# Edge ranking in 80 half-target buckets, and count matmuls of one half per chunk, in a two-layer graph network kernel

## What is computed

```python
edge_index = jnp.stack([src, dst])                    # 20625 edges, 625 nodes
xn = _layernorm(x, axis=-1)
x = x + _L0_gnn_ref(xn, edge_index, edge_type_8, ...) + _L0_mix_ref(xn[None], ...)[0]
x = x + _L0_ffn_ref(_layernorm(x, axis=-1)[None], ...)[0]
xn = _layernorm(x, axis=-1)
x = x + _L1_gnn_ref(xn, edge_index, ...) + _L1_mix_ref(xn[None], ...)[0]
x = x + _L1_ffn_ref(_layernorm(x, axis=-1)[None], ...)[0]
```

```python
for r in range(8):
    mask = (edge_type == r)
    sums = jax.ops.segment_sum(msgs * mask[:, None], dst, num_segments=n)
    cnt = jax.ops.segment_sum(mask, dst, num_segments=n)
    out = out + (sums / jnp.maximum(cnt, 1.0)[:, None]) @ weight[r]
```

## Time and profile before

| | |
|---|---|
| runs | 1880.85 us median of 3 (1880.52 to 1880.96) |
| profiled execution | span 1878.8 us, from first to last instruction |
| PE busy | 1794.9 us (96%) |
| PEld busy | 1477.4 us (79%) |
| DVE busy | 1023.3 us (54%) |
| ACT busy | 478.5 us (25%) |
| POOL busy | 701.1 us (37%) |

### The profile page before, as it was taken

How to read it: one execution, slowest core, us unless ns; L and a number is a source line. 1 busy time by engine, 2 the same in 40 slices (tenths; PEclk the granted TensorE clock), 3 DMA queues, 4 the chain that set the end, 5 groups by cost and what they waited for, 6 DMA issues and landing times.

```text
span 1878.8 us, 28666 instructions
## 1 busy us (share of the span) xinstructions
PE 1794.9 (96%) x9953; PEld 1477.4 (79%) x9953; DVE 1023.3 (54%) x2540; ACT 478.5 (25%) x1055; POOL 701.1 (37%) x609
## 2 busy tenths in 40 slices
PE   6999999999999999999999999954999999999999
PEld 4876689987777778787777887742899888878987
DVE  7888999997254543526354356786632224362311
ACT  3139956662010110101011145243100000111100
POOL 2110000003634435353534444200485552345862
PEclk9999999999999999999999999956999999999999
DMA  4532222224213121231313534110354351113322
GB/s 134 154 109 77 73 86 79 75 67 129 91 38 89 45 72 56 66 86 47 94 33 113 172 84 131 45 46 7 96 164 146 104 156 51 37 55 118 90 73 66
DMA packets 129282, 162.23 MB, mean 86 GB/s; under 512 B 14288, under 2 KB 75368, under 8 KB 128922
## 3 DMA queue, kind: packets, MB, share of 16 engines
q1 hardware_dynamic: 100848, 120.93, 21.5%
q10 hardware_dynamic: 22250, 23.53, 4.0%
q0 software_dynamic: 6080, 16.40, 2.9%
HBM read 135.51 MB, written 25.30 MB: 86 GB/s over the span
## 4 chain that ended last, share of the span: by engine, by line
PE 84%; DVE 6%; ACT 6%; issue 1%; DVEq 1%; DMA 1%; POOL 0%; ACTq 0%; SPq 0%
PE ps L367 22%; PE ps L368 22%; PE ps L369 21%; PE ps L1236 9%; PE ps L892 3%; ACT sc_col L838 2%; ACT sc_row L837 1%; PE ps L1201 1%; DVE w_lo L318 1%; PE ps L881 1%; PE ps L1156 1%; DMA nat<-in_x 1%; ACT w_hi L313 1%; PE ps L1183 1%; PE ps L1211 0%
## 5 line engine op out<-in xcount | busy, mean ns | idle before, releaser
L367 PE MATMUL ps<-w_hi,xt_hi 128*125 128x512 f32 x1320 | 539.0, 408 | 9.1 <-DVE xt_lo L549 3.5
L256 POOL TENSOR_TENSOR w_hi<-w_stage,zero 128x512 fp32r<-128x512 f32 x256 | 276.8, 1081 | 684.4 <-PE ps L369 670.0
L368 PE MATMUL ps<-w_lo,xt_hi 128*125 128x512 f32 x1320 | 523.0, 396 | 0.0
L369 PE MATMUL ps<-w_hi,xt_lo 128*125 128x512 f32 x1320 | 521.5, 395 | 0.0
L259 POOL TENSOR_TENSOR w_lo<-w_stage,w_hi 128x512 fp32r<-128x512 f32 x256 | 346.2, 1352 | 20.1
L367 PEld LDWEIGHTS ps<-w_hi,xt_hi 128*125 128x125 f32 x1320 | 246.6, 187 | 67.1 <-DVE xt_lo L549 4.3
L369 PEld LDWEIGHTS ps<-w_hi,xt_lo 128*125 128x125 f32 x1320 | 246.0, 186 | 63.3
L368 PEld LDWEIGHTS ps<-w_lo,xt_hi 128*125 128x125 f32 x1320 | 246.3, 187 | 53.5
L367 PE MATMUL ps<-xt_hi,w_hi 128*128 128x314 f32 x736 | 250.5, 340 | 1.3 <-DVE ring L2430 0.6
L369 PE MATMUL ps<-xt_hi,w_lo 128*128 128x314 f32 x736 | 225.9, 307 | 0.0
L368 PE MATMUL ps<-xt_lo,w_hi 128*128 128x314 f32 x736 | 225.7, 307 | 0.0
(11 more groups left out here) (392 smaller groups left out, 2390.2 us busy)
## 6 DMA issues: line engine op xcount, KB each, us to landing
w_stage<-in_stream SPq DMA_DIRECT2D x374, 256.0 KB, 2.7
pre<-ring POOLq DMA_DIRECT2D x30, 250.0 KB, 3.8
a_qt<-pre_t SPq DMA_DIRECT2D x18, 312.5 KB, 3.8
a_qt<-pre_t ACTq DMA_DIRECT2D x14, 312.5 KB
pre_t<-ring_t POOLq DMA_DIRECT2D x12, 312.5 KB, 2.8
pre_t<-ring_t ACTq DMA_DIRECT2D x12, 312.5 KB
a_vx<-pre SPq DMA_DIRECT2D x9, 312.5 KB
nat<-pre SPq DMA_DIRECT2D x2, 1250.0 KB
```

The costliest lines, as they stand in the source:

```text
L256: POOL.tensor_tensor(w_hi[:, q, :], w_stage[:, q % NST, :], zero[:].to_broadcast([128, 512]), ALU.add).then_inc(S("hi_done"), 1)
L367: PE.matmul(dst, l_hi, r_hi, start=first, stop=False)
L368: PE.matmul(dst, l_hi, r_lo, start=False, stop=False)
L369: return PE.matmul(dst, l_lo, r_hi, start=False, stop=last)
```

## The change

- A bucket is now relation, source tile and half of the targets (`SPLIT` = 314): 80 buckets (`NKEY`), rounded up to chunks of 128 slots, again 240 chunks. Targets are numbered within their half. A chunk's counts have 314 columns.
- Ranking: three buckets, 28 apart, share one row of `key_hot` as fields of 8 bits (weights 1, 256, 65536), so that table and running sum have 28 x 166 = 4648 elements. New are `key_weight` (`key_hot` times the edge's weight), the unpacking of sums, `ranks()` (rank of each edge within its partition, ahead of the evacuation of group 1), `rank_fields()`, and in `positions` 80 scalar operations (`key_start`, int16) in place of one addition and one multiplication of 6600 elements.
- Counts: for each chunk one `hot_col` of 314 targets and one count matmul of 314 columns; `hot_row` for four chunks at a time in one operation of 512 elements (`iota1_by4`), read by PE with a stride of four columns; the two chunks of a pair go to two banks (6 and 7, or 4 and 5) and are copied by one ACT operation of 2 x 314; two adds of 314 instead of one of 626; packed words of three chunks instead of four groups. DVE makes the hot_col of chunk c+4 ahead of the add of chunk c.

```diff
-GROUP = 256
-NGROUP = (EDGES + NBUCKET * (GROUP - 1)) // GROUP
-NCHUNK = 2 * NGROUP
+SPLIT = 314
+NKEY = 2 * NBUCKET
+FIELDS, NROW = 3, 28
+CHUNK = 128
+NCHUNK = (EDGES + NKEY * (CHUNK - 1)) // CHUNK
...
-        for b in (0, half):
-            DVE.tensor_tensor(key_hot[:, b:b + half], e_key[:].unsqueeze(1).to_broadcast([P, half, EC]),
-                              iota16[0:P, b:b + half].unsqueeze(2).to_broadcast([P, half, EC]), ALU.is_equal)
-            if b == 0:
-                split_low_dve(8, 11)
+        DVE.tensor_tensor(key_hot[:], e_row[:].unsqueeze(1).to_broadcast([P, NROW, EW]),
+                          iota16[0:P, 0:NROW].unsqueeze(2).to_broadcast([P, NROW, EW]), ALU.is_equal)
+        split_low_dve(8, 11)
+        DVE.drain()
+        DVE.tensor_tensor(key_weight[:], key_hot[:], e_weight[:].unsqueeze(1).to_broadcast([P, NROW, EW]), ALU.mult)
         evacuate(0)
...
+    def ranks():
+
+        DVE.tensor_tensor(scan[:], scan[:], key_hot[:], ALU.mult)
+        DVE.drain()
+        n = NROW
+        while n % 2 == 0:
+            n //= 2
+            DVE.tensor_tensor(scan[:, 0:n], scan[:, 0:n], scan[:, n:2 * n], ALU.add)
+            DVE.drain()
+        DVE.tensor_reduce(e_rank[:], scan[:, 0:n].rearrange("p b c -> p c b"), AX.X, ALU.add)
+        DVE.drain()
...
     def positions(evacuate):
-        DVE.tensor_tensor(scan[:], scan[:], b_off[:].unsqueeze(2).to_broadcast([P, NBUCKET, EC]), ALU.add)
-        DVE.tensor_tensor(scan[:], scan[:], key_hot[:], ALU.mult)
+        for b in range(NKEY):
+            DVE.tensor_scalar(key_start[:, b, :], e_key16[:], float(b), b_off[:, b:b + 1], ALU.is_equal, ALU.mult)
+            if b == NKEY // 2:
+                split_low_dve(24, 27)
...
+    def hist_hot(c):
+        if c % 4 == 0:
+            if c >= 8:
+                DVE.wait_ge(S("hi_pe"), c - 4)
+            DVE.tensor_tensor(hot_row[c // 4 % 2][:], iota1_by4[:],
+                              slot_row[:, c:c + 4].unsqueeze(1).to_broadcast([128, 128, 4]), ALU.is_equal)
+        if c >= 8:
+            DVE.wait_ge(S("hi_pe"), c - 7)
+        DVE.tensor_scalar(hot_col[c % 8][:], iota1_16[:, 0:SPLIT], slot_col[:, bass.ds(c, 1)], None,
+                          ALU.is_equal).then_inc(S("hi_dve"), 1)
+
+    def hist_copy(g):
+        b = pair_bank(g)
+        ALE.wait_ge(S("hi_pe"), 2 * g + 2)
+        if g >= 4:
+            ALE.wait_ge(S("hi_add"), 2 * g - 6)
+        ALE.activation(counts[g % 4][:], ps[0:P, b:b + 2, 0:SPLIT], ACT.Copy).then_inc(S("hi_main"), 1)
+
+    def hist_add(c, packed):
+        bucket = (packed >> (7 * (c % 3))) & 127
+        start = nc.s_assert_within((bucket >> 1) * NB + (bucket & 1) * SPLIT, 0, (NBUCKET - 1) * NB + SPLIT,
+                                   skip_runtime_bounds_check_because="a bucket's number is below NKEY")
+        DVE.wait_ge(S("hi_main"), c // 2 + 1)
+        if c:
+            DVE.wait_ge(S("hi_add"), c)
+        o = adj[:, bass.ds(start, SPLIT)]
+        DVE.tensor_tensor(o, o, counts[c // 2 % 4][:, c % 2, :], ALU.add).then_inc(S("hi_add"), 1)
...
         mk = bucket_counts(evacuate)
         split_low_dve(16, 21)
+        ranks()
         dense(1)
         mk = bucket_sums(mk)
         evacuate(1)
         split_low_dve(21, 24)
-        mk = group_buckets(mk)
+        rank_fields()
+        mk = chunk_buckets(mk)
```

More of the change, by code:

```diff
@@ L682, in build @@
     assert r_hot + sc_per * 1248 <= R_NAT + T * D * 4
[L683 to L688, removed]
+    slot_col = tmp("slot_col", [128, NCHUNK], F32, 1)
+    slot_row = tmp("slot_row", [128, NCHUNK], F16, 1)
+    hot_col = [tmp(f"hot_col{i}", [128, SPLIT], F16, 1) for i in range(8)]
+    hot_row = [tmp(f"hot_row{i}", [128, 128, 4], F16, 1) for i in range(2)]
+    zero16 = tmp("zero16", [P, 2 * NCHUNK], F16, 1)
+    iota1_by4 = at("iota1_by4", [128, 128, 4], F16, r_hot + sc_per * 1248)
+    assert r_hot + sc_per * 1248 + 1024 <= R_NAT + T * D * 4
+    counts = [at(f"counts{i}", [P, 2, SPLIT], I16, R_NAT + i * 1280) for i in range(4)]
     slot_ps = ps[:, 5, 0:2 * NCHUNK]
@@ L715, in bucket_counts @@
         DVE.tensor_scalar(e_key[:], ed_typ[:], float(T), None, ALU.mult)
+        DVE.scalar_tensor_tensor(e_col1[:, 0:EC], e_half[:], -float(SPLIT), e_col1[:, 0:EC], ALU.mult, ALU.add)
         DVE.drain()
@@ L811, in packed_buckets @@
         gflat = gcol[:].rearrange("o g j -> o (g j)")
[L812 removed]
+        DVE.tensor_scalar(gflat, ps[0:1, 6, 0:NCHUNK], -1.0, None, ALU.add)
         DVE.drain()
@@ L860, in hist_copy @@
-    def hist_copy(g, gm):
-        b4, b1 = group_banks(gm)
-        ALE.wait_ge(S("hi_pe"), 8 + 2 * g + 2)
-        ALE.wait_ge(S("hi_add"), g + 1)
-        ALE.activation(counts[gm][:, C1:NB], b1, ACT.Copy).then_inc(S("hi_rest"), 1)
-        ALE.activation(counts[gm][:, 0:C1], b4, ACT.Copy).then_inc(S("hi_main"), 1)
-    def hist_dve_add(g, gm, packed):
-        bucket = nc.s_assert_within((packed >> (6 * gm)) & 63, 0, NBUCKET - 1,
-                                    skip_runtime_bounds_check_because="a bucket's number is below NBUCKET")
-        DVE.wait_ge(S("hi_rest"), 2 + g + 1)
-        DVE.wait_ge(S("hi_main"), 2 + g + 1)
-        DVE.wait_ge(S("hi_add"), 4 + g)
-        o = adj[:, bass.ds(bucket * NB, NB)]
-        DVE.tensor_tensor(o, o, counts[gm][:], ALU.add).then_inc(S("hi_add"), 1)
@@ L877, in hist_pe_rest @@
[L877 to L893 removed]
+    LEAD_HOT = 4
@@ L895, in beside, with hist_pe @@
+    def hist_pe(g):
+        if g >= 2:
+            PE.wait_ge(S("hi_main"), g - 1)
+        if g == 1:
+            PE.wait_ge(S("bank_free"), (SC0 + SC_GROUPS + 1) * T)
+        for j in range(2):
+            c = 2 * g + j
+            PE.wait_ge(S("hi_dve"), c + 1)
+            PE.matmul(ps[0:P, pair_bank(g) + j, 0:SPLIT], hot_row[c // 4 % 2][:, 0:P, c % 4], hot_col[c % 8][:],
+                      start=True, stop=True).then_inc(S("hi_pe"), 1)
+    SC0, LEAD = 4, 6
     def beside(dense, evacuate, evacuate_half, load_bias):
@@ L923, in beside @@
         PE.sem_inc(S("sc_pe"), sc_per)
-        PE.sem_inc(S("hi_pe"), 6)
-        zero16 = hot_col[4][0:P, 0:128]
-        DVE.memset(zero16, 0.0)
-        DVE.memset(hot_col[5][0:P, 0:2 * NCHUNK], 0.0)
-        DVE.memset(slot[:, :, NCHUNK:NCHUNK + 4], 0.0)
-        for q in (6, 7):
-            DVE.memset(hot_col[q][:], 0.0)
-            DVE.memset(hot_row[q][:], 0.0)
+        DVE.memset(zero16[:], 0.0)
+        DVE.tensor_copy(iota1_by4[:], iota1_16[:, 0:128].unsqueeze(2).to_broadcast([128, 128, 4]))
         mk = sig(DVE.drain(), "dve_step")
         wait(PE, mk)
-        PE.matmul(slot_ps, zero16, hot_col[5][0:P, 0:2 * NCHUNK], start=True, stop=False)
+        PE.matmul(slot_ps, zero16[:, 0:128], zero16[:], start=True, stop=False)
         def scatter_step(i):
```

219 lines of the change are left out of this document (124 added, 95 removed).

## The result

The changed kernel takes 1972.08 us (median of 4 runs, 1970.87 to 1972.81), the kernel before, run beside it, 1880.68; the ratio is 1.0488 with a 95% interval from 1.0473 to 1.0503. The forecast said slower, with 1920 us and a range up to 1948: the direction held, the size did not. The measured loss is 91 us where 39 were forecast.

The account below looks back on a forecast made before the run. DVE was taken to set the count stage's pace, with PE close behind. Span 1878.8 + 12 (ranking) - 1 (before the count stage) + 29 (count stage) + 2.05 (outside the span) = 1920.9, stated as 1920 us; range 1885 to 1948.

Parts of the forecast that it names:

- Ranking and clock: Ranking stage: PE waits for late evacuations, then runs at a lower clock (+1.7 us); scatter starts 12 us later (6 to 18).
- The engines' share of the count stage: Count stage: DVE and PE, taken as engines alone, would allow some 150 us instead of 181.5.
- rival 1: Count stage: sequencer's work stays hidden, engines bind at 150 us; kernel 1861 us; chance 0.15.
- the period of 0.80 and 0.90 us: Count stage: time from add to add on DVE, 0.80 us without a load, 0.90 with one; mean 0.83.
- the high end, 0.85: Count stage: upper estimate of the period from add to add without a load, 0.85 us.
- 12 us that the forecast added for splits: Count stage: 32 w_lo splits on DVE are not covered between adds and lengthen the stage by 12 us.
- Rival 2: Count stage: sequencer's work half hidden, period 0.70 us, stage 179 us; kernel 1886 us; chance 0.07.
- Rival 3: Count stage: PE's clock drops and PE sets the pace for a quarter of the pairs; +20 us, 1940; chance 0.08.
- Rival 4: Ranking costs nothing, count stage as forecast; kernel 1909 us; chance 0.70 together with the main forecast.
- lower end of 1898: Whole kernel: low end, 1898 us, of the span 1898 to 1938 given for the main forecast.
- What would show it: Signs expected in the trace: count stage near 210 us, adds 0.8 apart, DVE near 60% busy, PE pausing some 9 us.
- The signs of being wrong: Count stage: adds at 0.6 us or PEclk low across it; ranking: key_start operations at 0.3 us each, +8 more.

Follow-up runs that it names:

- e5_resched: Changed kernel with DVE's ranking order changed: evacuation 1 ahead of the halvings in ranks(), evacuation 2 behind 65 key_start operations, splits moved to match; 1962.82 us.
- e2_static: Changed kernel with add addresses known when it is built: no register steps, no packed words loaded, wait kept, counts in wrong blocks; 1858.63 us.
- e3_load_once: Changed kernel with 2 packed-word loads instead of 80; most register steps fell away too, most counts land in wrong blocks; 1860.27 us.
- e1_regs_first: Changed kernel with each add's address computed into its own register ahead of the two waits, only base plus offset left behind; 1949.9 us.

## Why the prediction was right in direction and too small

**Ranking and clock: right, a little small.** These are rows of DVE's timeline around evacuation 1:

```profile
82.67 0.69 DVE L322 TENSOR_TENSOR w_lo<-w_stage,w_hi 128x512 fp32r<-128x512 f32 x1 [1.83 <-ACT w_hi L317]
83.28 4.99 DVE L799 TENSOR_TENSOR scan<-scan,key_hot 125x4648 f32<-125x4648 f32 x1
...
92.44 2.24 DVE L806 TENSOR_REDUCE e_rank<-scan 125x166 f32<-125x1162 f32 x1
94.85 3.08 DVE L480 TENSOR_TENSOR ring<-ps,bias_pre 125x512 f32<-125x512 f32 x5 [0.17 <-issue]
```

Evacuation 0 starts at 55.3 (forecast 55.4), evacuation 1 at 94.85 (92.9), and PE waits 11.9 us in two places, here the longer one in its timeline:

```profile
95.69 0.76 PE L371 MATMUL ps<-w_hi,xt_hi 128*125 128x512 f32 x1 [11.10 <-DVE ring L480]
```

The window behind it, columns as in the earlier trace rows:

```profile
96.00:100.00 4.00, 4.00 (x10) 3.11 (x10) 3.92 (x9) 0.00 (x0) 2.49 (x5) 0.50 0.64 182
```

Its 0.50 is the granted clock, 1.2 GHz, behind PE's pause, as forecast. The sum up to the first add was +11 and came out at +13.6; ranks() itself took 11.4 us (forecast 11.3) and ended 1.8 us late, because the split ahead of it ended at 83.36 and not at 81.6. The key_start operations took 14.0 us for 80, 0.175 each, where I had 0.19. e5_resched shows the mechanism: with ranks() moved out of the way, PE's waits for evacuations fall from 11.9 to 1.4 us.

**The engines' share of the count stage: right.** "150 us as engines" was 148 to 149 in e2_static and e3_load_once, and rival 1's total of 1861 us is theirs to within 2.4 us. Its condition alone was wrong: the steps are not hidden.

**The step that failed: the period of 0.80 and 0.90 us.** In the forecast's terms:

| term | forecast | trace |
|---|---|---|
| add of 314 | 0.32 | 0.32 |
| wait for the add before | 0.16 | 0.11 ahead of the steps + 0.05 behind them |
| five register steps | 0.32 | 0.46 |
| plain period | 0.80 | 0.94 |
| period with a load | 0.90 | 1.23 |

The five steps are the mis-sized term. The fused step of the earlier trace rows takes 0.057, and the forecast priced both fused steps of the new address by it; they take 0.08 and 0.13. (That more arithmetic is folded into them would explain it; no run shows the reason.) And 0.03 us stand between any two steps, 0.12 in all, where 0.07 was allowed. Even the high end, 0.85, lay below what was measured. The period with a load falls into four parts: 0.66 from the start of the add until load, test and assertion are over (353.40 to 354.06; 0.60 allowed), 0.12 until the first register step (nothing allowed, because the add had ended at 353.72: the waiting step and the gaps around it are there all the same), 0.40 for four steps, and 0.05 until the add (0.30 allowed for these two).

For 160 periods without a load and 80 with one, 0.14 and 0.33 more make 22 + 26 = 48 us, and the stage took 49 more than forecast. That the sum closes so well is in part luck. The 12 us that the forecast added for splits are some 5 in the trace; the other 7 are periods longer than their kind, above all beside loads of up to 0.99 us: the 46 plain periods with a load are 1.32 in the mean, not 1.23.

The table of the four count stages shows that a price of the load had no single value: 28 us beside steps behind a wait, 9 without. The forecast added it to a chain that it had made too short.

**Rival 2** (half hidden) needed a period of 0.70. **Rival 3** (the clock): the granted clock did fall, to 0.86 from 464 to 519 us, but it set nothing. There were 28 adds in 344 to 374 us at a clock of 1.00 and 27 in 464 to 494 at 0.85. The 20 us that it was to cost don't appear. **Rival 4** did not come about (+13.6 ahead of the first add). The forecast's lower end of 1898 is not the sum of its own terms either: +6, -1 and +17 give 1903.

**What would show it**: adds 0.8 apart (0.94), DVE idle between hot_col and add (0.40 us, put down to "issue"), DVE's share near 60% (64%), PE waiting for hot_col more than for copies (67.3 us against 32.9 at the count matmuls' weight loads in the waits), a pause of some 9 us ahead of group 2 (11.1): all in kind as named. The stage near 210 us was 259.4. The signs of being wrong named adds at 0.6 us, a low clock and slow key_start operations, and none of them came: nothing in the list looked for a period above 0.83.

**Where the wait stands.** Ahead of each add the program has two waits: for the copy, and for the add before. The second is a step of DVE's sequencer by itself in the changed kernel (L957) and in e2_static (L955) alike, 239 times, once for every add but the first. These are the rows of the two lines, in this order:

```profile
L957 DVEq EVENT_SEMAPHORE  x239: 21/21/21, 259.6 to 518.1; - x120
```

```profile
L955 DVEq EVENT_SEMAPHORE  x239: 21/21/21, 258.2 to 405.7; - x120
```

So the wait has not moved; what differs is what stands behind it. In e2_static an add starts at 301.09 and takes 0.31, and the next one starts at 301.53: 0.13 behind the end of the one before, which is the whole price of the bare wait, and 0.21 behind the start of the hot_col between, which is DVE's own pace (in e3_load_once the add behind the hot_col at 351.30 starts 0.21 later too, with the add before it over since 351.05). In the changed kernel five register steps stand between the waiting step and the add, and 0.13 becomes 0.62. The difference of 0.49 is their 0.46 and one gap of 0.03. Wait and steps are two terms of one sum, as the forecast had them, and the earlier trace rows, with a step behind its wait, fits it too; only the size of the second term was wrong.

The Trainium skill has the distinction that lies under this, in "Perfetto Trace Analysis" (Sequencer Loop, and the timelines for an engine: Sequencer-only Instruction and DVE / Act Engine Instruction): an instruction for the engine waits in a queue, and the sequencer goes on to the next, while an instruction that the sequencer executes itself is waited for by the sequencer. The trace of the changed kernel agrees with both halves: the load behind a hot_col in DVE's queue starts at 353.5, before that hot_col itself does (353.64), and no register step of an address starts before the waiting step ahead of it is over.

## What to carry to other kernels

Before cutting an operation into pieces, count for each piece what the issuing engine's sequencer must do by itself (address steps, register loads, tests, waits) and compare that sum, gaps included, with the engine time of the piece: where the engine time is the smaller, the engine stands idle (here 0.40 us in a plain period), and its busy share falls while the kernel gets slower. Where an address comes from data, have the wide engine prepare the finished offset and let the sequencer only unpack it; that was worth 87 us here, lighter loads included, while moving the same steps ahead of the wait was worth 22. And an engine that works between two uses of a PSUM bank should serve the evacuation first: here 11.4 us of ranks() ahead of it became a wait of 11.1 us for TensorE, and the other order gave 9.3 us back.

## What the runs showed of the hardware

- A fused register step has no fixed price: 0.046 us (base plus offset), 0.057, 0.08, 0.13, and 0.18 to 0.22 for the range test of a loaded word. A single ALU_OP is 0.04. Between two register steps 0.03 us go by, beside a waiting step 0.05.
- A register load from memory occupies DVE's sequencer for 0.30 us, in a few cases longer (up to 0.99 in the changed kernel, 1.20 in e1_regs_first), while the engine goes on with what it has. What it costs depends on what waits behind it.
- A wait of DVE for its own last but one instruction is a step of its sequencer, 0.02 us long. The next add starts 0.13 us behind the end of the instruction waited for where nothing else stands between (e2_static), which a hot_col of 0.21 hides; the first register step starts 0.11 behind that end (changed kernel).
- A wait in the trace is put down to the last semaphore before it: 21.6 us "<- ACT" were register steps, which a longer lead did not touch.
